# Window attention: two score maxima in one VectorE operation, both banks of transposed probabilities in one ScalarE copy

## The reference

```
q, k, v = (groupnorm(x) in 7 x 7 windows of 8 x 8 pixels) @ W_qkv + b_qkv
logit   = window means of q times window means of k ;  r_idx = the 4 best windows of each
k_sel, v_sel = k, v of the 4 chosen windows            # 256 keys for 64 queries, 8 heads of 16
attn = softmax(q_h * SCALE @ k_sel^T) ;  o = attn @ v_sel
x = x + (o + lepe(v)) @ W_o + b_o                      # lepe: a 3 x 3 depthwise convolution
```

## Time and profile before

| what | value |
|---|---|
| median of 3 runs | 3797.24 us (3796.34 to 3798.78) |
| the profiled execution, its own time | 3793.72 us |
| its span in the trace | 3792.0 us |
| TensorE busy | 3522.8 us, 93% |
| VectorE busy | 2374.0 us, 63% |
| ScalarE busy | 2142.8 us, 57% |
| GpSimd busy | 1655.4 us, 44% |

### The profile page before, as it was taken

The page is one execution under the profiler, slowest core; times in us unless marked ns, Lnnn a source line. Parts: engine busy times, 40 slices in busy tenths (PEclk is TensorE's granted clock), DMA queues, the critical chain, the costliest instruction groups (busy, mean ns, idle before and its releaser), DMA issues. The chain is left out here.

```text
span 3792.0 us, 107529 instructions
## 1 busy us (share of the span) xinstructions
PE 3522.8 (93%) x31974; PEld 2993.2 (79%) x31974; DVE 2374.0 (63%) x6251; ACT 2142.8 (57%) x5921; POOL 1655.4 (44%) x2575
## 2 busy tenths in 40 slices
PE   6989898989989898969999999999999969979999
PEld 4656565656656565659999999999999969979998
DVE  4868687777868686853333333333333349988898
ACT  4969788787879797954443333333333324435554
POOL 2636364554636363730003333333334436646665
PEclk8999999999999999989999999999999989989999
DMA  6232222323132323211110000000002100000000
GB/s 213 71 96 74 90 80 75 87 61 110 49 113 58 108 63 98 73 66 50 50 55 1 0 0 0 0 0 0 0 6 61 61 26 1 1 14 35 35 35 34
DMA packets 202875, 194.44 MB, mean 51 GB/s; under 512 B 35744, under 2 KB 191136, under 8 KB 199456
## 3 DMA queue, kind: packets, MB, share of 16 engines
q1 hardware_dynamic: 171168, 177.15, 15.0%
q10 hardware_dynamic: 31360, 12.87, 1.2%
HBM read 123.30 MB, written 66.58 MB: 50 GB/s over the span
## 5 line engine op out<-in xcount | busy, mean ns | idle before, releaser
L196 PE MATMUL bank<-h,w_hh 128*128 128x128 f32 x8032 | 933.9, 275 | 0.0
L196 PEld LDWEIGHTS bank<-h,w_hh 128*128 128x128 f32 x8032 | 917.2, 192 | 0.0
L241 ACT ACTIVATE h<-bank,bg 128x128 f32<-128x128 f32 x1008 | 370.0, 367 | 818.7 <-PE bank L196 818.6
L1579 ACT ACTIVATE Pr<-bank,nmx 128x256 f32<-128x256 f32 x1568 | 722.6, 477 | 122.4 <-DVE nmx L1682 108.0
L1516 POOL TENSOR_TENSOR Pr<-Pr,rden 128x768 f32<-128x768 f32 x392 | 574.7, 1466 | 383.3 <-DVE rden L1749 383.3
L1682 DVE TENSOR_REDUCE nmx<-bank 128x1 f32<-128x256 f32 x1568 | 557.0, 416 | 210.1 <-PE bank L1854 206.4
L287 DVE SCALAR_TENSOR_TENSOR inp<-bank,b_in,tz 128x256 f32<-128x256 f32 x196 | 85.8, 479 | 698.2 <-ACT tz L224 698.2
L1508 POOL COPY kg<-kT 128x64 f32 x1568 | 312.6, 243 | 392.4 <-DMA row<-ix 303.6
L1865 PE MATMUL bank<-ident,Pr 128*128 128x128 f32 x3136 | 450.5, 285 | 3.7 <-POOL Pr L1516 2.1
L1588 ACT ACTIVATE PT<-bank 128x512 f32<-128x512 f32 x784 | 427.3, 604 | 39.7 <-PE bank L1865 36.6
L1854 PE MATMUL bank<-kg,qT 32*128 32x256 f32 x3136 | 399.8, 440 | 31.6 <-POOL kg L1508 22.9
(11 more groups left out here) (261 smaller groups left out, 6500.2 us busy)
## 6 DMA issues: line engine op xcount, KB each, us to landing
v_rows<-v_padded SPq DMA_DIRECT2D x168, 232.0 KB, 3.4
vg<-v_windows SPq DMA_DIRECT2D x1176, 32.0 KB, 2.1
first_gates<-gate_sums SPq DMA_DIRECT2D x28, 512.0 KB, 2.6
gate_sums<-first_gates SPq DMA_DIRECT2D x28, 512.0 KB, 3.5
v_padded<-vpad SPq DMA_DIRECT2D x56, 232.0 KB, 2.4
X<-in_x SPq DMA_DIRECT2D x8, 1568.0 KB, 15.1
vg<-v_windows ACTq DMA_DIRECT2D x392, 32.0 KB, 2.2
x_backup<-X SPq DMA_DIRECT2D x8, 1568.0 KB, 6.0
```

The costliest lines, as they stand in the source:

```text
L196: ins = pe.matmul(bank[m][:, tt * COLS:(tt + 1) * COLS], w_hh[:, k, m * 128:(m + 1) * 128], prev[:, k, :], start=False, stop=(k == NH - 1) ...
L241: act.activation(h[:, 2 * q + tt, m, :], bank[m][:, tt * COLS:(tt + 1) * COLS], ACT.Tanh, bias=bg[:, 0, m:m + 1]).then_inc(s_h, 1)
L1579: act.activation(Pr[:, par, j, :], bank[j][:, 0:KEYS], ACT.Exp, bias=nmx[:, par, j:j + 1], accum_out=den[:, par, j:j + 1])\
```

## The change

The eight PSUM tensors of one bank each become one tensor of eight banks, `banks`, and `bank[i]` becomes its slice, so that an operation can read two banks. `maxes` then takes two pairs in one `tensor_reduce`, 128 x 2 x 256 to 128 x 2: it waits for the scores of the second pair of the two, and counts its semaphore up by 2. `turned` copies banks 4 and 5 in one activation of 128 x 1024 and counts up by 2. The waiting sides are not edited: `exps` still waits for the count of each pair, and `attend` for the count of both copies.

```diff
-        bank = [psm(f"bank{i}", [128, 512]) for i in range(8)]
+        banks = psm("bank", [128, 8, 512])
+        bank = [banks[:, i, :] for i in range(8)]
...
-                            for i in range(2):
-                                act.activation(PT[:, par, i * 512:(i + 1) * 512], bank[4 + i][:], ACT.Copy)\
-                                    .then_inc(s_Tc, 1)
+                            act.activation(PT[:, par, :].rearrange("p (b k) -> p b k", b=2), banks[:, 4:6, :], ACT.Copy)\
+                                .then_inc(s_Tc, 2)
...
-                            for j in range(PAIRS):
-                                dve.wait_ge(s_S, (n * P2 + w + 1) * PAIRS + j + 1)
-                                dve.tensor_reduce(nmx[:, par, j:j + 1], bank[j][:, 0:KEYS], AXX, ALU.max, negate=True)\
-                                    .then_inc(s_mx, 1)
+                            for j in (0, 2):
+                                dve.wait_ge(s_S, (n * P2 + w + 1) * PAIRS + j + 2)
+                                dve.tensor_reduce(nmx[:, par, j:j + 2], banks[:, j:j + 2, 0:KEYS], AXX, ALU.max, negate=True)\
+                                    .then_inc(s_mx, 2)
```

## The result

The change made the kernel slower. Its median is 3818.61 us (3811.91 to 3824.13, 4 runs) against 3796.79 us (3792.56 to 3798.78, 4 runs) for the kernel before: ratio 1.0058, with a 95% interval of 1.0039 to 1.0077, that is about +22 us (15 to 29 by the interval). The forecast was 3791.8 us, and its range ended at 3807. The profiled execution of the change took 3811.91 us with a span of 3810.2, so +18.2 us on the span before.

What follows compares the result with a forecast made beforehand. A loop through several engines, loop B, was taken as the bound. Chains at -1.12 and -0.24 us an image, middle -0.68, gave -5.4 us over 8 images: median 3791.8 us, range 3776 to 3807.

Steps and rivals of the forecast that it cites:

- loop B: Two-window cycle from transposes through scores, maxima, exponentials, copies and `attend`; 6.17 us, taken to set the pace.
- a turn with a branch: Two windows including ScalarE's loop branch, where its queue still holds the exponential: -0.06 for dispatch, -0.06 for copy, -0.12 us.
- The one chain: Of two interleaved window chains, the one with every branch: 16 ordinary turns and 8 with a branch, -1.12 us an image.
- the start of the first exponential: First exponential of a window, counted from the transposes: 2.47 us, where ScalarE's queue allowed 2.42 before; 0.05 us later.
- reduction over two banks: Merged maxima on VectorE: one reduction of two pairs takes 0.68 us, bounds 0.67 and 0.75.
- wait for the second pair's scores: Merged maximum on VectorE starts later because it needs two pairs' scores: 0.01 us, at most a few hundredths.
- "a dispatch" less ahead of the DMA issue: ScalarE's queue has one instruction fewer ahead of its load and DMA: saves 0.06 us, between 0 and 0.14.
- merged copy, copies to `attend`: One ScalarE copy in place of two overlapping ones shortens the way to `attend` by 0.06 us, bounds 0 and 0.08.
- loop A: One-window cycle of copies, `attend` and transposes: 3.06 us, to become 3.00 and no longer matter.
- The slack of GpSimd's product: Product after VectorE's reciprocals has slack, so reciprocals about 0.09 us sooner count only in windows where it holds the transposes.
- The late first maximum (slower): Rival: reduction of 0.75 us or more delays the exponential 0.12 us; +11.5 us, 3808.7; decides from 0.69. Chance 0.15.
- Loop A was the bound: Rival: the one-window copy cycle sets the pace, so each window gains the full 0.06 us; -23.5 us, 3773.7. Chance 0.2.

Runs made afterwards that it cites:

- max_merged_by2: Kernel before with only the maxima merged, their semaphore raised by 2; copies stay separate. 3809.77 us against 3795.63, ratio 1.0034.
- copy_merged_by1: Kernel before with only the copies merged, their semaphore raised by 1 and waits counted accordingly; maxima stay single. 3790.4 us against 3795.63, ratio 0.9982.
- late_wait: Kernel before with four single maxima; only the first and third also wait for the next pair's scores. 3800.97 us against 3795.63, ratio 1.0017.
- both_merged_by1: The whole change, but both semaphores raised by 1 and waits counted accordingly. 3798.04 us against 3796.15 for the kernel before, ratio 1.0004.
- fourth_on_sync: Kernel before with the fourth DMA of each window's values and its register load moved from ScalarE to SyncE. 3879.46 us against 3796.15, ratio 1.021.
- last_pair: Kernel before with only the third and fourth pairs' maxima merged, raised by 1; first two stay single. 3795.91 us against 3793.15, ratio 1.0005.

## Why the prediction was wrong

**Where the extra time went.** With the measured distances in the prediction's own sum: an ordinary turn of loop B is +0.165 - 0.06 = +0.105 us in place of -0.01, a turn with a branch +0.04 - 0.06 = -0.02 in place of -0.12. The one chain then loses 16 x 0.105 - 8 x 0.02 = 1.5 us an image, the other 24 x 0.105 = 2.5, the middle is 2.0, and 8 images make +16 us. The trace has +18. The step that failed is the start of the first exponential: "The first exponential could then start, counted from the transposes, at 2.47 us". It is 2.59 in the timeline. The terms, in us:

| step of the prediction | forecast | measured |
|---|---|---|
| reduction over two banks | 0.68 | 0.687 |
| wait for the second pair's scores | 0.01 | 0.042 |
| raise by 2 on the maxima | not seen, 0 | 0.069 |
| raise by 2 on the copies: copy start | not seen, 0 | 0.049 |
| "a dispatch" less ahead of the DMA issue | -0.06 | 0 by 1, +0.05 by 2 |
| merged copy, copies to `attend` | -0.06 | 1.34 to 1.28 |

**How far the sum itself can be trusted.** That +16 comes so near to +18 is in part luck. For max_merged_by2 the same sum gives 8 x (16 x 0.165 + 24 x 0.165) / 2 = +26 us, and the run had +14; for copy_merged_by1 8 x 24 x -0.06 = -12, and it had -5 to -7; for late_wait 0, and it had +5. It charges the maxima too much. And it has nearly nothing for the raise on the copies, which moves loop A, the loop that "no longer matters": that one was to fall from 3.06 to 3.00, and its windows in the change take 3.055.

**The raises.** "counts its semaphore up by 2" stood in the description of the change and had no price in the sum. It is the larger error: some 20 of 22 us by both_merged_by1 against the change. By single parts it is about 5 us for the maxima (1.0034 less 1.0021) and 13 for the copies (1.0016 less 0.9982; TensorE's wait for the product is in this figure), 18 together.

**The second pair's wait.** The prediction read its price from the time that the first passes of all four pairs take together, 0.50 us less 0.44 to 0.48. But the ends of matmuls are modelled there, and no row showed when the second pair's scores release a maximum. late_wait measured 0.042.

**The slack of GpSimd's product.** "GpSimd's product has slack in loop B" held for the change: the reciprocals come 2.23 us behind the first maximum in place of 2.33, as forecast, and the product is what the transposes wait for last in 15 windows, where it was 64 before. It does not hold for any later maximum. In late_wait, where the maximum moves by 0.04 us and the reciprocals with it (2.33 behind it), the product comes last in 102 windows, and the kernel loses 5 us with its first exponential in place. That this chain is what costs them is read from the traces; no run delayed the product alone.

**The busy times.** VectorE's was to fall by 119 us and ScalarE's by 71; they fell by 30 and 20. The prediction took the durations of all single operations together, but those that follow at once overlap and count once: the 1568 single maxima are 557.0 us busy, not 1568 x 0.416 = 652. It had no part in the forecast of the time.

**The rivals.** "The late first maximum (slower)" was the case that came, by its place and its sign: from 0.69 us on it would decide. The reduction is 0.687, so its condition was met not by length but by a late start. It gave 3808.7, 10 us short of the measured time; the raise on the copies, which this rival did not have either, is of that size. "Loop A was the bound" was put at 0.2 and -23.5 us. By itself the merged copy is worth -5 us by the medians (-7 by the ratio), so loop A sets the pace only in some windows. Together with last_pair it is -17. What was right: ScalarE's queue as the holder of the first exponential and the maximum's slack (fourth_on_sync), both durations, and that there was no gain of half a microsecond in the copies.

**What stays open.** How the 13 us between the two merged copies divide. The start of the copy moves by 0.049 us, which is 0.049 x 392 = 19 us if every window felt it and 24 x 8 x 0.049 = 9 us if only each turn of loop B did; TensorE's wait for the product adds 0.075 us in some 50 windows, up to 4 us. And whether the fourth fetch on a queue that is in time would bring the 0.2 us at the exponential.

## What to carry to other kernels

When two operations are merged, the semaphore should still go up by 1, and the waiting sides should count the merged operations: here a raise by 2 took the wait off the instruction, which put its start 0.05 to 0.07 us later each time, as much as the merged copy saved (0.06). After such an edit, look in the records at which instruction carries each wait, on the waiting engines too; the counts alone moved one on TensorE. A merge also makes the first consumer wait for the whole pair, so the first of a row is left alone and the last ones are merged, where nobody waits. And single changes to a kernel with two bounds close together say little: the merged last pair gave nothing alone, and 0.3% on top of the merged copy.

## What was not expected of the hardware

- The reduction with a raise by 2 has its wait in an instruction of its own, 784 in this run, and starts 0.069 us later. On ScalarE the wait moved into the wait instruction ahead, with no additional one, and the copy started 0.049 us later. Only the records of the trace showed it.
- TensorE's wait for GpSimd's product stood on a register instruction with the counts by 2 and on the weight load with counts by 1; where the product came last, the transposes started 0.130 us behind its end in the one form and 0.055 in the other.
- A reduction over two PSUM banks took 687 ns, two over one bank each 0.335 + 0.416 = 0.75 us; it started no later (0.774 us behind the scores in both kernels that wait for the second pair).
- ScalarE's copy of 1024 columns out of two banks took 1029 ns, and two of 512 columns 1.08 to 1.09 us, since the second begins before the first has ended.
- A loop body of 24 windows on ScalarE in place of 6 came with a stop of 3.46 us behind its branch and 101 more packets in the instruction queue.
